# Eight graph batches through four layers: the third-layer matrix dropped, batch 1's first layer moved under batch 0's attention, row squares moved to ScalarE

## The reference

```python
# layer 0
y = einsum('nm,bmf->bnf', adj, x) + x
y = einsum('bnf,fo->bno', y, weight) + bias
y = y / maximum(sqrt(sum(y * y, axis=2)), 1e-12)
# layer 1: attention, with adj as the mask
A = (x @ q) @ (x @ k).T / sqrt(128)
A = exp(tanh(A / 8) * 8) * adj
out = (A / sum(A, -1)) @ x @ v
# layer 2: rank-one gates and adj
res = si[:, :, None] + sj[:, None, :] + adj * w_r + g_b
out = (res @ x) @ weight + bias
# layer 3: Chebyshev basis
d = sum(adj, -1) ** -0.5
L = eye - d[:, None] * adj * d[None, :]
out = relu(sum over k of ([eye, L, 2 L L - eye][k] @ x) @ weight[k] + bias)
```

## Time and profile before

| | us |
|---|---|
| median of 3 runs | 725.47 (725.03 to 727.37) |
| the profiled execution's own time | 725.35 |
| its span, first to last instruction | 723.2 |
| mean granted clock of TensorE | 0.968 |
| busy: TensorE | 640.1 |
| busy: VectorE | 597.2 |
| busy: ScalarE | 385.1 |
| busy: GpSimd | 72.5 |

### The profile page before, as it was taken

The page is one execution under the profiler, slowest core; times in us unless marked ns, Lnnn a source line. Parts: engine busy times, 40 slices in busy tenths (PEclk is TensorE's granted clock), DMA queues, the critical chain, the costliest instruction groups (busy, mean ns, idle before and its releaser), DMA issues. The chain is left out here.

```text
span 723.2 us, 17684 instructions
## 1 busy us (share of the span) xinstructions
PE 640.1 (89%) x7606; PEld 489.1 (68%) x7606; DVE 597.2 (83%) x1495; ACT 385.1 (53%) x531; POOL 72.5 (10%) x49
## 2 busy tenths in 40 slices
PE   5727946889999999999999999998999999869895
PEld 5714623566976698667966697668866796637895
DVE  6667978997989798988989898988889897879525
ACT  3668756743458245934486255914494446613402
POOL 0020011001200120011200120011100220020102
PEclk9959977999999999999999999999999999989998
DMA  8010000000100020001100020002000010000101
GB/s 308 2 29 1 2 16 15 1 1 2 31 1 2 1 60 2 1 2 29 34 1 2 1 61 2 1 2 60 2 1 2 1 31 2 1 1 2 31 2 59
DMA packets 20013, 14.55 MB, mean 20 GB/s; under 512 B 864, under 2 KB 18912, under 8 KB 19936
## 3 DMA queue, kind: packets, MB, share of 16 engines
q1 hardware_dynamic: 18816, 12.91, 5.6%
q10 hardware_dynamic: 1120, 0.52, 0.3%
HBM read 9.24 MB, written 4.19 MB: 19 GB/s over the span
## 5 line engine op out<-in xcount | busy, mean ns | idle before, releaser
L239 POOL TENSOR_TENSOR small<-small,minus_half 128x8 f32<-128x8 f32 x39 | 68.1, 1750 | 636.5 <-DVE small L533 320.9
L387 ACT ACTIVATE att<-r,coef 128x1024 f32<-128x1024 f32 x64 | 70.5, 1102 | 53.5 <-PE r L1115 52.9
L1243 PE MATMUL av<-vhi,p_hi 128*128 128x129 f16 x512 | 89.7, 220 | 9.0 <-DVE p_lo L806 8.7
L1246 PE MATMUL av<-vhs,p_lo 128*128 128x129 f16 x512 | 89.5, 220 | 0.0
L1245 PE MATMUL av<-vlo,p_hi 128*128 128x128 f16 x512 | 89.5, 219 | 0.0
L801 DVE TENSOR_TENSOR att<-att,adjT 128x1024 f32<-128x1024 f32 x64 | 78.0, 1218 | 7.6 <-ACT att L389 7.6
L806 DVE SCALAR_TENSOR_TENSOR p_lo<-p_hi,att 128x1024 f16<-128x1024 f16 x64 | 77.9, 1218 | 0.0
L1113 PE MATMUL r<-gr,lap 128*128 128x128 f16 x448 | 75.8, 219 | 0.0
L1115 PE MATMUL r<-gr,lap 128*128 128x128 f16 x448 | 75.8, 219 | 0.0
L1114 PE MATMUL r<-gr,lap 128*128 128x128 f16 x448 | 75.8, 219 | 0.0
L1115 PE MATMUL r<-xq,lap 128*128 128x128 f16 x448 | 75.4, 219 | 0.0
(11 more groups left out here) (304 smaller groups left out, 1925.8 us busy)
## 6 DMA issues: line engine op xcount, KB each, us to landing
x<-in_x SPq DMA_DIRECT2D x8, 512.0 KB, 4.2
lap<-in_adj SPq DMA_DIRECT2D x8, 512.0 KB, 8.7
out<-outb SPq DMA_DIRECT2D x7, 512.0 KB, 3.5
out<-att SPq DMA_DIRECT2D x1, 384.0 KB, 2.8
x<-in_L_gnn_weight ACTq DMA_DIRECT2D x1, 192.0 KB, 11.7
b_bc<-in_L_gnn_bias SPq DMA_DIRECT2D x3, 64.0 KB, 11.3
out<-att SPq DMA_DIRECT2D x1, 128.0 KB, 2.7
x<-in_L_gnn_q ACTq DMA_DIRECT2D x1, 64.0 KB, 2.9
```

Source lines behind the costliest of these rows:

```text
L239: return nc.gpsimd.tensor_tensor(dst, src, minus_half[:], ALU.pow)
L387: nc.scalar.activation(att[:, s], (r1, r0)[t % 2][:], ACT.Tanh, scale=c_tanh).then_inc(S["th"], 1)
L1243: mm(acc, p_hi[:, s, chunk(j)], vhi[:, t, 0:D + 1], start=(t == 0 and j % 3 == 0), stop=False, skip_group_check=True)
L1246: l_ = mm(acc, p_lo[:, s, chunk(j)], vhs[:, t, 0:D + 1], start=False, stop=(t == C - 1), skip_group_check=True)
```

## The change

- `lap`, its scales and its sixteen copies are gone. `apply_laplacian` reads `a_hi` and `a_lo`; the scale of a row, minus the square of `dis`, is put into r and q when they are split (`r_scale`, `q_scale`). `r_hi`, `r_lo`, `q_hi` and `q_lo` therefore become four instructions of 128 columns for each half instead of one of 512.
- The memory of `adj_rows` is used, once the rows are consumed, for a second set of `x1T`, `g`, `vhi`, `vhs`, `vlo`, and for r's pair. `x1` and `x2` become one tile per batch, two of them in turn.
- Batch 1's x is loaded early, into `outb`. Its product with the adjacency is placed in batch 0's first layer, its projection, norm and transposes in batch 0's attention. Batch 0's layer-1 residual, norm, gate steps and x2's split move from before batch 1's attention into it; batch 0's gate sums and the second half of adj times x2 follow batch 1's attention.
- From batch 2 on the row squares of layer 0 are summed by ScalarE (`row_squares`, four accumulating Square instructions a half), in place of eight statistics and three small operations on VectorE.
- In the adjacency stage VectorE makes one `adjT` copy instead of two, the weights' maxima come after chunk 0, and TensorE's first product is placed behind chunk 2's transposes and a wait for these maxima.
- The iterations are written as `start`, `front(i)` and `back(i)`; for batches 2 to 6 the order on TensorE stays as it was.

```diff
-DVE_COPIES = 2
+DVE_COPIES = 1
...
             def r_hi(z, b, h):
                 act.wait_ge(S["r_mm"], 2 * b + h + 1)
-                copy(z.gr[:, 0, half(h)], r2[:, half(h)], R_DOWN).then_inc(S["r_hi"], 1)
+                for j in range(h * C // 2, (h + 1) * C // 2):
+                    l_ = copy(z.gr[:, 0, chunk(j)], r2[:, chunk(j)], r_scale[:, j:j + 1])
+                l_.then_inc(S["r_hi"], 1)
...
-                copy(cd(z.xq[:, 0])[:, half_chunks(h)], z.pq[:, half_chunks(h)]).then_inc(S["q_hi"], 1)
...
+                for j in range(h * C // 2, (h + 1) * C // 2):
+                    l_ = copy(z.xq[:, 0, chunk(j)], z.pq[:, j], q_scale[:, j:j + 1])
+                l_.then_inc(S["q_hi"], 1)
...
+            def row_squares(b, h):
+
+                act.wait_ge(S["e0_c"], row_links(b) + 2 + h)
+                for j in range(h * C // 2, (h + 1) * C // 2):
+                    l_ = nc.scalar.activation(tmp[:, j], xas[b % 2][:, j], ACT.Square, accum_out=small[:, 4, 0, j:j + 1])
+                l_.then_inc(S["norm_sq"], 1)
...
+            def back(i):
+                last = i >= 2
+                act.wait_ge(S["y0_mm"], 2 * (i + 1))
+                x0_hi(i + 1)
+                y2_hi(i - 1, 1)
+                act.wait_ge(S["p2_mm"], i)
+                y0_hi(i + 1, 0, r1[:, half(0)])
+                norm(2, i - 1, x3, V_CHUNKS)
+                y0_hi(i + 1, 1, r1[:, half(1)])
+                row_squares(i + 1, 0)
+                if last:
+                    act.wait_ge(S["o_mm"], 2 * (i - 1))
+                for h in range(2):
+                    x3t_hi(z_all, i - 1, h)
+                for h in range(2):
+                    r_hi(z_all, i - 1, h)
+                row_squares(i + 1, 1)
+                if last:
+                    act.wait_ge(S["q_lo"], 2 * (i - 1))
+                p_copy(z_all, i - 1)
...
-                split_lo(z.gr[:, 1, half(h)], r2[:, half(h)], R_DOWN, z.gr[:, 0, half(h)], "r", 2 * b + h + 1)
+                dve.wait_ge(S["r_hi"], 2 * b + h + 1)
+                for j in range(h * C // 2, (h + 1) * C // 2):
+                    l_ = stt(z.gr[:, 1, chunk(j)], r2[:, chunk(j)], r_scale[:, j:j + 1], z.gr[:, 0, chunk(j)],
+                             ALU.mult, ALU.subtract)
+                l_.then_inc(S["r_lo"], 1)
...
-                        l_ = split_product(dst[:, chunk(j)], lap[:, 0, m, chunk(j)], lap[:, 1, m, chunk(j)],
+                        l_ = split_product(dst[:, chunk(j)], a_hi[:, m, chunk(j)], a_lo[:, m, chunk(j)],
...
+                for t in range(1, C):
+                    mask(0, t)
+                    p_lo_part(0, t - 1)
+                    if t == 1:
+                        rows.y_half(0, r2)
+                        rows.y_half(1, r2)
+                    if t == 2:
+                        rows.stats_half(0)
+                        rows.stats_half(1)
+                        rows.arg()
+                    if t == 3:
+                        row_scales()
+                    if t == 4:
+                        rows.residual()
+                    if t == 5:
+                        ln_begin(0, 1, xas[1])
+                    if t == 6:
+                        gate_weights()
+                        ln_shift(0, 1)
+                        ln_norm(0, 1, xas[1])
...
-                if c == 1:
+                if c == 2:
                     pe.wait_ge(S["x_lo"], 1)
                     pe.wait_ge(S["iu_ok"], 1)
-                if c == 3:
                     pe.wait_ge(S["w_max"], 5)
                     mm(m7[:, 3 * P:3 * P + 5], ones[:], wmax[:], start=True, stop=True).then_inc(S["w_sum"], 1)
-                if c >= 1:
-                    adj_x0_chunk(c - 1)
...
+                if c >= 2:
+                    adj_x0_chunk(c - 2)
+            adj_x0_chunk(C - 2)
...
+            def start():
+
+                pe.wait_ge(S["w_red"], 6)
+                layer0_half(0, 0, r1)
+                adj_x0_chunk(C - 1)
+                row_max_sum(1)
+                layer0_half(0, 1, r1)
+                pe.wait_ge(S["x_lo"], 2)
+                adj_x0(0, 0, C, m7, 0)
+                adj_x0(1, 0, 4, av[:, 2], 0)
+                x1_t(0, r1)
+                adj_x0(1, 4, 6, av[:, 2], 0)
+                pe.wait_ge(S["w_red"], 10)
+                g_product(0, r2)
+                adj_x0(1, 6, C, av[:, 2], 0)
+                v_product(0, r1)
...
+                attend(1, 6)
+                attend(1, 7)
+                pe.wait_ge(S["y2_lo"], 1)
+                sum_x2(m7)
+                sums_w2(m7, 0)
+                pe.wait_ge(S["l2_c"], 1)
+                for part in range(4, 8):
+                    adj_x2_part(0, part)
```

More of the change, by code:

```diff
@@ L462, in _ @@
+            back(1)
+            for i in range(2, B - 1):
+                front(i)
+                back(i)
+            front(B - 1)
+            norm(1, B - 1, xas[(B - 1) % 2], V_CHUNKS)
             y2_hi(B - 2, 1)
@@ L823, in finish_stats, with back @@
+            def back(i, l2_ch):
+                last = i >= 2
+                xa, xn = xas[i % 2], xas[(i + 1) % 2]
+                sj_ch = Count(dve, S["sj_c"], i, 5)
+                y2_lo(i - 1, 1)
+                if last:
                     dve.wait_ge(S["f_c"], i - 1)
                     ln_stats(3, i - 2, outb)
-                if last:
-                    for h in range(2):
-                        end_sum(i - 2, h)
-                if nxt and prev and not is_first(i, 1):
-                    x0_max(i + 1)
@@ L887, in body @@
                     ln_arg(3, i - 2)
[L888 to L901 removed]
+                row_sums(i)
@@ L995, in body @@
-                if cur:
-                    for k_ in range(4):
-                        sj_step(sj_ch, i, k_)
-                    x2_lo(i)
-            iterations(dve, body)
+                rows = Rows(i + 1)
+                rows.begin()
+                rows.y_half(0, r1[:])
+                y0_lo(i + 1, 1, r1[:, half(1)])
+                for h in range(2):
+                    x3t_lo(z_all, i - 1, h)
+                rows.y_half(1, r1[:])
+                for h in range(2):
+                    r_lo(z_all, i - 1, h)
@@ new lines, in back @@
+                rows.arg()
+                dve.wait_ge(S["e1a"], i + 1)
+                ln_stats(1, i, xa)
+                rows.residual()
+                ln_begin(0, i + 1, xn)
+                u_part(z_all, i - 1)
+                q_part(z_all, i - 1, 0)
+                ln_shift(0, i + 1)
+                ln_norm(0, i + 1, xn)
+                ln_arg(1, i)
+                q_lo(z_all, i - 1, 0)
+                x1t_lo(i + 1, r1)
+                q_part(z_all, i - 1, 1)
+                ln_shift(1, i)
@@ L1002, in _ @@
+                q_lo(z_all, i - 1, 1)
+                ln_norm(1, i, xa)
+                g_lo(i + 1, r2)
+                v_lo(i + 1, r1)
+                for k_ in range(4):
+                    sj_step(sj_ch, i, k_)
+                x2_lo(i)
+            back(1, start())
+            for i in range(2, B - 1):
+                back(i, front(i))
+            front(B - 1)
             row_sums(B - 1)
             for j in range(C):
-                l_ = attention_residual(j)
+                l_ = attention_residual(B - 1, j)
@@ new lines, in scores, with next_scores @@
+            def scores(i, t):
+                xt, g = xts[i % 2], gs[i % 2]
+                dst = (r1, r0)[(t + (i == 0)) % 2]
+                for h in range(2):
+                    l_ = split_product(dst[:, half(h)], xt[:, 0, chunk(t)], xt[:, 1, chunk(t)],
+                                       g[:, 0, half(h)], g[:, 1, half(h)], True, True)
+                l_.then_inc(S["s_mm"], 1)
+            def next_scores(i, t):
+                pe.wait_ge(S["th"], i * C + t - 1)
+                scores(i, t)
@@ new lines, in attend @@
+            def attend(i, t):
+                vhi, vlo, vhs = vhis[i % 2], vlos[i % 2], vhss[i % 2]
+                pe.wait_ge(S["pl"], i * C + t + 1)
+                s = t % RING
+                for j in range(C):
+                    o = (j % 3) * AVW
+                    acc = av[:, j // 3, o:o + D + 1]
+                    mm(acc, p_hi[:, s, chunk(j)], vhi[:, t, 0:D + 1], start=(t == 0 and j % 3 == 0), stop=False,
+                       skip_group_check=True)
+                    mm(acc[:, 0:D], p_hi[:, s, chunk(j)], vlo[:, t, :], start=False, stop=False, skip_group_check=True)
+                    l_ = mm(acc, p_lo[:, s, chunk(j)], vhs[:, t, 0:D + 1], start=False, stop=(t == C - 1),
+                            skip_group_check=True)
+                l_.then_inc(S["av_mm"], 1)
@@ new lines, in front @@
+                adj_x2(2)
+                next_scores(i, 5)
+                attend(i, 2)
+                adj_x2(3)
+                next_scores(i, 6)
+                attend(i, 3)
+                next_scores(i, 7)
+                attend(i, 4)
+                if nxt:
+                    adj_x2(4)
+                    attend(i, 5)
```

(17 more changed lines are left out.)

973 lines of the change are left out of this document (465 added, 508 removed).

## The result

The changed kernel takes 728.59 us (median of 10 runs, 728.07 to 730.9), the kernel before 725.53 (10 runs, 725.0 to 727.37): ratio 1.0045, 95% interval 1.003 to 1.0059. It is slower by 0.45%. The profiled execution took 728.07, its span is 725.8.

What follows compares the result with a forecast made beforehand. TensorE was taken as full in middle batches (77.21 of 79.10 us), with 20 us idle in the start. From 725.35: -13.0 start, +5.2 clock, +10.5 middle batches, +2.3 tail gave 730.4 us; range 716 to 743, its own case 727 to 735.

Steps and rivals of the forecast that it cites:

- -13.0: Start: batch 1's first score comes 22 us earlier, 9 are given back before batch 0's W2 product, minus 13.0 us.
- W2 at 151, first score 101 to 103: Start, predicted sign: batch 0's W2 product near 151, batch 1's first score near 101 to 103, clock's 5.2 us included.
- twice 2.6: Start: two new TensorE holes each bring a clock fall costing 2.6 us, plus 5.2 in all, bounds 0 and 8.
- The adjacency stage, price 0: Start: despite TensorE's wait for the weights' maxima, the stage ends at 34.8, as before within 0.3 us.
- Rival (a): Start: all 22 us of lead at batch 1's first score reach W2, 721.4 us; chance 0.13.
- Rival (c): Start: the clock never falls, 725.2 us, no change; chance 0.13.
- A middle batch, 1.75 predicted: Loop: x1 transposes 0.85 us late plus q 0.9 make 1.75 a batch, 10.5 in six batches.
- What stands last before the Laplacian: Middle batch: pq's copy ends at 260.14, the low part and u's product at 259.8; Laplacian 1.6 us late.
- Tail, 2.3 predicted: Tail, batches 6 and 7: r's chain 0.9 us each and q's steps 0.5, plus 2.3 us.
- (b): Middle batch: no new wait, squares and short steps fit beside TensorE, 716.3 us; chance 0.09.
- (d): Loop and tail: heavy ScalarE steps, squares 0.49 and copies 0.394 us, 4.5 a batch, 748.6 us; chance 0.09.
- (e): Loop: Square isn't in the loaded table, one 1.28 us table load per batch, 738 us; chance 0.05.

Runs made afterwards that it cites:

- e4: Changed kernel with r and q split in halves of 512 columns by constants, third layer's row scale left out: 715.6 us, ratio 0.9881.
- e3: Changed kernel with the row squares of all batches back on VectorE, short steps kept: 738.21 us, ratio 1.0185.
- e5: Changed kernel with row squares on VectorE and r and q in 512-column halves, row scale left out, only the new start left: 718.98 us, ratio 0.992.
- e6: Changed kernel with the copy of p placed ahead of the second four squares on ScalarE: 734.48 us, ratio 1.0141.
- e7: Changed kernel with the second half of r and q first row-scaled by VectorE, then split in 512 columns: 729.16 us, ratio 1.0058.
- e11: Changed kernel with q alone in 512-column halves by a constant, q's row scale left out: 723.68 us, ratio 0.9996.
- e1: Changed kernel with filler matmuls that nothing needs in the start's two holes on TensorE (78 and 70): 725.49 us, ratio 1.001.
- e8: Changed kernel with filler matmuls in TensorE's holes all through the start: 726.55 us, ratio 1.0016.
- e9: Changed kernel with e8's fillers, 88 more in the tail's 5.45 us hole, and q's second half as in e7: 724.08 us, ratio 0.9986.
- e10: Kernel before with 205 filler matmuls in each of its two 12.3 us holes and 88 in the tail's: 720.04 us, ratio 0.9947.
- e12: Kernel before with row squares on ScalarE from batch 2 on, and e10's fillers: 718.27 us, ratio 0.9895.
- e2: Changed kernel with the adjacency stage as in the kernel before: 729.23 us, ratio 1.0059.

## Why the prediction was right, and where two errors cancelled

The sum was -13.0 + 5.2 + 10.5 + 2.3 = +5.0; in the traces it is -7.6 (W2) + 8.6 (iteration 1 and five periods, six times 1.43) + 1.7 (tail) = +2.7, which gives 728.05 for the profiled run's 728.07.

These are figures of one execution of each kernel. Each row below is one trace, or several that agree, cut into four stretches of the start, us:

| | from the product with the maxima to the projection | to batch 0's first tanh | to batch 1's first score | to W2 | W2 at |
|---|---|---|---|---|---|
| changed kernel | 21.41 | 23.30 | 39.33 | 48.94 | 151.48 |
| e4 | 20.98 | 23.07 | 39.76 | 48.92 | 151.76 |
| e3, e5, e6, e7, e11 | 20.17 to 20.62 | 24.40 to 24.56 | 39.31 to 39.33 | 50.60 to 50.62 | 152.55 to 154.13 |
| e1, two holes filled | 18.58 | 22.43 | 39.32 | 50.60 | 149.53 |
| e8, all holes filled | 18.56 | 22.43 | 39.78 | 48.92 | 148.43 |

The first three rows are seven kernels with the same instructions up to W2. Their W2 differs by 2.7 us, and the changed kernel's is the earliest; its profiled run, 728.07, is also the fastest of its ten.

1. **W2 at 151, first score 101 to 103.** Both came out (151.48, 102.54). But the two terms behind it were each too large. Without clock falls the lead is 11.2 (an estimate put together from two traces): the first score at 98.93 in e1, then the 48.94 that the changed kernel takes to W2, 147.87, against 159.09. I had 13.0: 0.9 of the difference lies ahead of the first score (98.0 predicted), 0.8 behind it (48.1). The falls cost 3.6, not 5.2: the first hole 2.73 (the projection, e1 against the changed kernel; 2.6 was predicted), the second hole 0.88 (3.61 less 2.73 at the first score). In the other six like traces, held against the filled ones, the first costs 1.6 to 2.4, the second 0.6 to 2.1. The step that failed is "twice 2.6". In the second hole the low clock lasted from 41.6 to 48.4, and the product for batch 1 began only at 44.98, so half of the fall lay in the hole itself; and with the hole filled the x1 transposes wait 0.59 for VectorE, which takes back some of the gain. Where TensorE does not set the end, a fall costs nothing: batch 0's attention takes 39.3 with falls (89.4 to 92.8 in the changed kernel, 90.6 to 97.4 in e3) as it takes 39.8 without (e8). That the two errors, 1.8 and 1.6, cancelled to 0.2 is luck, and so is that the trace to compare with was an early one: with the W2 of the five like kernels the start would have given back 1.1 to 2.7 more.
2. **The adjacency stage, price 0.** The prediction's working doesn't close: 17.5, eight products, five groups of transposes and a projection end at 34.45 by its own figures, 34.8 is written, and the old end is 36.91 by the same sentence, so "within 0.3" does not follow; the forecast then went on with 37.0. What the price is can't be told apart from the spread: with filled holes the projection was at 37.18 to 37.31 (e1, e8, e9), in the kernel before at 36.06, and with the same instructions up to there at 37.62 in e10 and e12.
3. **Leads are given back in batch 1's attention.** Right: 48.94 us from its first score to W2, predicted 48.1, before 39.13. Rival (a), that the lead holds, fell.
4. **The clock.** Rival (c) fell: mean clock 0.50 in 18.5 to 23 and in 45 to 48. What the prediction did not have is that the short waits around the sums can bring it down too (in seven of nine traces that have them, e1 and e2 among these), and the waits of batch 0's attention (e9 at 67.1; the changed kernel at 72.3 and 89.4).
5. **A middle batch, 1.75 predicted, 1.43 measured.** The pieces, counted from the first tanh: the Laplacian 1.34 late instead of 1.62; of that the x1 transposes absorbed 0.77, exactly as worked out; q added 0.84 to 0.89 instead of 0.9 (e11). The mis-sized term is the first: the r product is 0.19 late instead of 0.3, the eight copies with row scale are followed after 2.01 instead of 2.15, the four squares after 1.17 instead of 1.24, the copy took 0.04 more. Priced singly: an accumulating Square with its read has a pitch of 0.29, predicted 0.31.
6. **What stands last before the Laplacian.** Right: pq's copy, by 0.22 instead of 0.34 (e6). The other arm is so close behind it that moving the copy wins no more than that.
7. **Tail, 2.3 predicted, 1.7 measured** (122.65 us from the last batch's first tanh to the end, before 120.95). Two things are in it. Behind the hole the clock stayed low for 3.3 us of TensorE's work, in the kernel before for 5.0, so the product with `w_sb` that follows comes 54.98 after the first tanh instead of 55.69. From there to the end it is 67.7 instead of 65.3, 2.4 more, close to the 2.3. With long steps (e4) the waits of 0.39 and 0.80 ahead of u's products are gone, and that stretch is back at 65.3.
8. **Rivals (b), (d), (e).** No wait-free batch, no heavy steps (0.29 a square, 2.01/8 = 0.25 a copy, not 0.49 and 0.394), and the only ACT_TABLE_LOAD is the one at the start:

```profile
3.89 1.28 ACT L285 ACT_TABLE_LOAD   x1 [3.89 <-issue]
```

The Trainium skill, page "VectorE: DVE Perf Modes", section on the TRN2 errata, asks for long tiles because each instruction pays the SBUF latency. The traces agree for q, which VectorE reads from SBUF: four steps of 128 took 1.14 us, 512 columns 0.69. With r's steps, which are read from PSUM, e4 prices the short steps at 12 to 13 us for this kernel, more than the new start brings (5.7 us, e5).

What stays open: which of several like waits brings the clock down. The Trainium skill, page "TensorE: Matmul & The Clock Gate", section "What's actually happening", gives half rate after an idle stretch; both long holes here agree, but behind the short ones it fell in one execution and not in another. The executions of one kernel spread by 2.8 us (728.07 to 730.9), as much as W2 differs between the seven like kernels. No run here tells what decides it, and for the executions that were not profiled it isn't shown that the clock makes their spread.

## What to carry to other kernels

Where an engine's step lies on a chain with no slack, splitting it in four for a per-row operand costs what four fixed parts cost, each batch again: price that against what it buys, here a lead that comes once, in the start. Moving work off the busy engine is worth trying by itself; here it gained in every setting, and more the tighter the chain. A lead in the start counts only as far as it is still there where the steady loop begins. And compare positions in more than one execution: here like instructions ended up to 2.7 us apart.

## What the hardware showed unexpectedly

- The granted clock fell to half behind waits as short as 0.91 and 0.58 us in seven traces (e1, e2, e3, e5, e6, e7, e11; the falls begin between 141.7 and 146.3), and didn't behind the same two waits in the changed kernel and e4; behind a wait of 2.21 us it fell in e9 and not in e8.
- Low clock from 113.3 to 123.5 in the changed kernel cost nothing (48.94 us to W2, as in e9 with the clock at 1.00), while a shorter fall in a stretch of back-to-back matmuls cost 1.7 us (141.7 to 145.1 in e1).
- A wait can hide in a row without idle time: in a stream of matmuls that start 0.06 us apart and last 0.22, the step of 0.28 in front of the Laplacian was a wait of 0.22 (e6).
- Filler matmuls in a hole keep the clock up at most places, but where it falls anyway they run at half rate themselves and delay what stands behind them.
